# Both outer rows of a sampled attention summed on VectorE, row weights computed on GpSimd

## The reference, cut to what is computed

```python
x = x + _L0_conv_ref(_gn(x), Wq, Wk, Wv, off_w, off_b, attn_w, attn_b, Wo)
x = x + _L1_conv_ref(_gn(x), ...)

# in _L0_conv_ref: 8 heads of 8 channels, K2 = 9 taps
v = jnp.einsum('oc,nchw->nohw', Wv, x)
offsets = _conv2d(x, off_w, off_b)                    # 3x3, 144 channels
aw = jax.nn.sigmoid(_conv2d(x, attn_w, attn_b))       # 3x3, 72 channels
xp = (gx + 1.0) * 0.5 * (W - 1)                       # the pixel plus its offset
yp = (gy + 1.0) * 0.5 * (H - 1)
sampled = corner(y0, x0, wy0 * wx0) + corner(y0, x1, wy0 * wx1) + corner(y1, x0, wy1 * wx0) + corner(y1, x1, wy1 * wx1)
head_out = jnp.einsum('nhckxy,nhkxy->nhcxy', sampled, awr)   # summed over the taps k
return jnp.einsum('oc,nchw->nohw', Wo, combined)
```

## Time and profile before

| | us |
|---|---|
| Median of 3 runs (151.33 to 152.0) | 151.58 |
| Profiled execution, device time | 151.03 |
| Its span in the profile | 149.2 |
| Mean granted clock of TensorE, share of full | 0.976 |

### The profile page before, as it was taken

How to read it: one execution, slowest core, us unless ns; L and a number is a source line. 1 busy time by engine, 2 the same in 40 slices (tenths; PEclk the granted TensorE clock), 3 DMA queues, 4 the chain that set the end, 5 groups by cost and what they waited for, 6 DMA issues and landing times.

```text
span 149.2 us, 3269 instructions
## 1 busy us (share of the span) xinstructions
PE 129.2 (87%) x1395; PEld 111.3 (75%) x1395; DVE 110.5 (74%) x198; ACT 57.4 (38%) x102; POOL 18.5 (12%) x27
## 2 busy tenths in 40 slices
PE   4966399999999899999999998899887999797790
PEld 3654399998898889999899896687655667465460
DVE  5429895095459999799998999998757297965701
ACT  3009539837950768007880128012030317021100
POOL 8941120000000000000018000000003001030100
PEclk9999659999999999999999999999999999999999
DMA  3980000009964000000000000000000000000033
GB/s 95 271 152 0 0 0 4 0 15 256 244 120 108 19 7 0 0 0 4 0 0 0 0 4 0 0 0 4 0 2 4 4 0 4 0 4 0 0 75 70
DMA packets 6672, 5.48 MB, mean 37 GB/s; under 512 B 4656, under 2 KB 5938, under 8 KB 6658
## 3 DMA queue, kind: packets, MB, share of 16 engines
q1 hardware_dynamic: 5986, 4.26, 12.0%
q10 hardware_dynamic: 672, 1.02, 2.7%
HBM read 2.85 MB, written 0.52 MB: 23 GB/s over the span
## 4 chain that ended last, share of the span: by engine, by line
PE 50%; DVE 25%; issue 9%; DMA 6%; ACT 5%; SPq 1%; POOL 1%; POOLq 0%; DVEq 0%
PE bank L990 10%; PE bank L1009 9%; PE bank L982 8%; PE bank L1034 7%; DVE prod L742 7%; DMA prod<-in_w_off 6%; DVE part L769 3%; DVE x_t L861 3%; PE bank L1164 3%; PE bank L1131 3%; PE bank L959 2%; DVE wy L777 2%; DVE pooled L867 2%; DVE bn L580 2%; PE bank L943 2%
## 5 line engine op out<-in xcount | busy, mean ns | idle before, releaser
L742 DVE TENSOR_TENSOR prod<-hat,wy 128x1440 f32<-128x1440 f32 (+3 forms) x25 | 27.3, 1159 | 0.0
L769 DVE TENSOR_TENSOR part<-v,bank 128x1280 f32<-128x1280 f32 (+3 forms) x20 | 21.7, 1109 | 7.1 <-PE bank L1034 3.5
L1009 PE MATMUL bank<-cst,prod 128*128 128x128 f32 (+3 forms) x189 | 22.3, 272 | 0.8 <-DVE prod L742 0.8
L1034 PE MATMUL bank<-cst,part 128*128 128x128 f32 x168 | 21.1, 274 | 1.8 <-DVE part L769 1.4
L1009 PEld LDWEIGHTS bank<-cst,prod 128*128 128x128 f32 (+3 forms) x189 | 20.7, 131 | 1.4 <-DVE prod L742 1.0
L1034 PEld LDWEIGHTS bank<-cst,part 128*128 128x128 f32 x168 | 18.3, 140 | 3.2 <-DVE part L769 3.0
L943 PE MATMUL bank<-ones_r 128*128 128x512 f32 x67 | 18.5, 428 | 2.1 <-POOL w_pair L370 2.1
L990 PE MATMUL bank<-w_cross,g_cross 128*128 128x216 f32 x144 | 19.9, 285 | 0.0
L990 PEld LDWEIGHTS bank<-w_cross,g_cross 128*128 128x128 f32 x144 | 18.6, 203 | 0.0
L982 PE MATMUL bank<-w_pair,g_pair 128*128 128x216 f32 x96 | 15.3, 301 | 3.7 <-ACT g_cross L430 3.7
L943 PEld LDWEIGHTS bank<-ones_r 128*128 128x128 f32 x67 | 13.3, 207 | 4.9 <-POOL w_pair L370 2.1
(11 more groups left out here) (101 smaller groups left out, 154.9 us busy)
## 6 DMA issues: line engine op xcount, KB each, us to landing
v<-v SPq DMA_DIRECT2D x2, 480.0 KB, 6.2
v<-v SPq DMA_DIRECT2D x2, 448.0 KB, 5.9
prod<-in_w_off ACTq DMA_DIRECT2D x1, 486.0 KB, 7.0
prod<-in_w_off SPq DMA_DIRECT2D x1, 486.0 KB, 8.8
w_s<-in_w SPq DMA_DIRECT2D x4, 72.0 KB, 4.4
wc_s<-in_wc SPq DMA_DIRECT2D x2, 144.0 KB, 3.4
wp_s<-in_wp SPq DMA_DIRECT2D x4, 72.0 KB, 2.5
x_b<-in_x SPq DMA_DIRECT2D x1, 256.0 KB, 4.9
```

The source lines that it names most:

```text
L742: return nc.vector.tensor_tensor(prod[:, 0:K2 * CELLS * cx].rearrange("p (k q s) -> p q k s", k=K2, s=cx)[:, q0:q0 + nd], hat[:, c % 2, d0 ...
L769: nc.vector.tensor_tensor(part[:, n % PARTS, 0:nd, 0:cv].rearrange("p d (q e) -> p d q e", e=HD), moved, weights.unsqueeze(3).to_broadcast ...
L1009: last = nc.tensor.matmul(out_ps[0:size, b * P:(b + 1) * P], prod[:, at:at + size], ident, start=(b == 0 and t == 0), stop=(b == n - 1 and ...
L1034: last = nc.tensor.matmul(comb_bank[:, j * P:(j + 1) * P], part[:, n % PARTS, d, j * P:(j + 1) * P], ident, start=(m == 0 and d == 0 and j ...
```

## The change

- Rows 0 and 4 are both summed over their taps on DVE (`OWN_ROWS`, six cells). The reduction is replaced by four additions: taps 4 to 7 onto 0 to 3, taps 2 and 3 onto 0 and 1, tap 1 onto 0, and tap 8 with the sum into `cell`. The first three run in place in `prod`, each waiting for the one before.
- TensorE has two groups of tap sums. The projection of the chunk before stands between the transposes back of the two groups.
- `APPLY` is (4, 0, 2, 1, 3) in chunks 0 to 3 and stays (4, 2, 1, 3, 0) in chunk 4. The middle rows wait for the cells of both groups.
- The row weights `wy` of chunks 1 to 4 are computed by GpSimd once the weights `hat` are there and the second apply of the chunk before has ended; chunk 0's stay on DVE. DVE waits for them behind the edge reduction. GpSimd's clearing for the second block comes behind the last of them.
- On ScalarE all five distances and the far test of the next chunk come before the copies of the groups; the weights `hat` still come behind them.

```diff
+APPLY = ((4, 0, 2, 1, 3),) * (NC - 1) + ((4, 2, 1, 3, 0),)
-GROUPS = ((0, 8, 2), (8, 15, 3), (15, 18, 4))
-OWN_ROW = 4
-APPLY = (4, 2, 1, 3, 0)
+GROUPS = ((0, 8, 2), (8, 15, 3))
+SUMMED = 15
+OWN_ROWS = ROWS[3:]
+OWN = CELLS - SUMMED
...
+        def row_weights(engine, c):
+
+            x0, w = CHUNKS[c]
+            cx = w * HEADS
+            ck = K2 * cx
+            return engine.tensor_tensor(
+                wy[:, :, 0:ck].rearrange("p d (k q) -> p d k q", k=K2),
+                hat[:, c % 2, :, ck:2 * ck].rearrange("p d (k q) -> p d k q", k=K2),
+                mod[:, :, x0:x0 + w, :].rearrange("p k x h -> p k (x h)").unsqueeze(1).to_broadcast(
+                    [P, ND, K2, cx]), ALU.mult)
...
             nc.gpsimd.memset(wp_s[:, :, :, :], 0.0).then_inc(wp_zero, 1)
-            pool.wait_ge(off_ps, NC)
+            for c in range(1, NC):
+                pool.wait_ge(hat_ready, c + 1)
+                pool.wait_ge(mod_ready, c + 1)
+                pool.wait_ge(part_ready, ND * (c - 1) + len(OWN_ROWS))
+                row_weights(nc.gpsimd, c).then_inc(wy_ready, 1)
...
-            distances(1, 0, 1)
             for c in range(NC):
                 if c:
                     evacuate(c - 1)
-                    if c + 1 < NC:
-                        distances(c + 1, 0, 1)
+                if c + 1 < NC:
+                    distances(c + 1, 0, ND)
+                    far_tests(c + 1)
                 for g in range(len(GROUPS)):
                     copy_sums(c, g)
-                    if c + 1 < NC:
-                        distances(c + 1, g + 1, g + 2)
                 if c + 1 < NC:
-                    distances(c + 1, ND - 1, ND)
                     hats(c + 1)
...
-                for i in ROWS[:-1]:
+                ve.wait_ge(wy_ready, c + 1)
+                for i in ROWS[:3]:
                     product(i).then_inc(prod_ready, 1)
-                product(OWN_ROW).then_inc(hat_used, 1)
+                product(OWN_ROWS[0])
+                product(OWN_ROWS[1]).then_inc(hat_used, 1)
...
-                own_sum = tick(nc.vector.tensor_reduce(
...
+                taps = prod[:, 0:K2 * CELLS * cx].rearrange("p (k s) -> p k s", k=K2)[:, :, SUMMED * cx:]
+                link(nc.vector.tensor_tensor(taps[:, 0:4], taps[:, 0:4], taps[:, 4:8], ALU.add))
+                link(nc.vector.tensor_tensor(taps[:, 0:2], taps[:, 0:2], taps[:, 2:4], ALU.add))
+                link(nc.vector.tensor_tensor(taps[:, 0], taps[:, 0], taps[:, 1], ALU.add))
+                own_sum = tick(nc.vector.tensor_tensor(cell[:, :, 0:cx],
+                                                       taps[:, 0].rearrange("p (q s) -> p q s", s=cx),
+                                                       taps[:, 8].rearrange("p (q s) -> p q s", s=cx), ALU.add))
...
                 tap_sum(c, 0)
                 tap_sum(c, 1)
                 cells_back(c, 0)
-                tap_sum(c, 2)
-                cells_back(c, 1)
-                cells_back(c, 2)
                 if c:
                     y0(c - 1)
+                cells_back(c, 1)
```

## The result

| | before | changed |
|---|---|---|
| Median, us (4 runs each) | 151.46 | 154.8 (154.14 to 155.62) |
| Ratio, 95% interval | | 1.0264 (1.0156 to 1.0373) |
| Profiled execution, us | 151.03 | 154.14 |
| Its span, us | 149.2 | 152.3 |
| Mean granted clock | 0.976 | 0.955 |

A forecast was written before the change was run, and what follows sets the result against it. TensorE ends last in chunks 1 and 2, DVE in chunk 3. Chunk 3's products 2.1 us late, less 0.15, plus 0.3 in chunk 4, make 2.3 us: 151.58 + 2.3 = 153.9 us, range 151.3 to 156.6.

The forecast's parts named there:

- GpSimd's product of 1440 elements: Row weights of chunks 1 to 3 on GpSimd: 3.4 us each, against 1.65 on DVE.
- Work caught by the lower clock, its cost: TensorE behind chunk 0's gap: 4.2 us of work at the lower clock, costing 2.1 us.
- Products to second apply, chunk 4: Chunk 4: second apply 6.1 us behind the products, held by TensorE, where it was 5.76; 0.3 more.
- Part 4: ScalarE's five distances and far test ahead of the copies: TensorE stands still 3.7 us in chunk 0 and the clock falls.
- TensorE's lateness at chunk 1: TensorE free for chunk 1's tap sums at 52.1 instead of 48.26: 1.7 us late column plus 2.1 for the clock.
- All behind it is unchanged: Everything behind chunk 4's 0.3 us delay to the end of the kernel was to take the same time.
- Rival (b): Clock falls again in chunk 2's 1.9 us gap: another 2 us of TensorE time, 155.9 us; chance 0.10.
- Chunk 1's products: On DVE, they start at 47.2 instead of 45.8, behind GpSimd's product and the edge reduction.
- Rival (a): Clock stays at full through chunk 0's new gap: 2.1 us less, about 152.0 us; chance 0.22.
- Rival (c): Copies don't hold TensorE, DVE's period of 16.1 us counts: 2.5 us less, 149.1 us; chance 0.11.
- Rival (d): GpSimd's product outlasts its 4.8 us cover; at 6.5 us chunks 1 to 3 start later, near 157 us; chance 0.07.
- The lock between DVE and GpSimd: Between chunks, only the edge reduction (0.4 us) is held behind GpSimd's product; the three applies from PSUM are free.

The follow-up runs named there:

- experiment 1: Changed kernel with ScalarE's distances laid between the copies of the tap sums again, as in the kernel before: 149.81 us, ratio 0.986 to the kernel before.
- experiment 2: Kernel before with one part of the change alone, all five distances and the far test ahead of the copies: 160.81 us, ratio 1.0549.
- experiment 3: Changed kernel with 14 warming products in TensorE's gap before the first transpose back of chunk 0: 151.58 us, ratio 1.0016.
- experiment 8: Kernel of experiment 1 with shifted rows of v fetched in order 4, 0, 1, 3 and 8 instead of 10 warming products before chunk 4: 149.97 us.
- experiment 6: Changed kernel with the distances laid between the copies in chunk 0 alone: 151.02 us, ratio 0.9954.
- experiment 7: Changed kernel with the distances laid between the copies in chunks 1 to 3 alone: 151.23 us, ratio 0.9992.
- experiment 12: Kernel of experiment 1 once more, with more runs: 150.01 us, ratio 0.9862 to the kernel before, 12 runs.
- experiment 9: Kernel before with 17 instead of 10 warming products ahead of chunk 4: 152.49 us, ratio 1.0113.
- experiment 10: Changed kernel with 7 instead of 4 warming products between the two group means behind the last residual: 155.34 us, ratio 1.0135.
- experiment 11: Kernel of experiment 1 with 7 instead of 4 warming products between the two group means: 150.41 us, ratio 0.9886.
- experiment 4: Changed kernel with the row weights of every chunk back on DVE: 154.56 us, ratio 1.024.

## Why the prediction was right, point by point

The forecast for the median was 153.9 us, 2.3 above the kernel before; measured were 154.8 and 3.3 (3.1 between the profiles). Sign, mechanism and order of size are right, the size in part by luck; the parts are these.

| Step | forecast | measured |
|---|---|---|
| GpSimd's product of 1440 elements | 3.4 us | 3.28 |
| Products of chunk 1 start | 47.2 | 47.34 |
| First column behind the copies, chunk 0 | 40.25 | 40.08 |
| Work caught by the lower clock, its cost | 4.2, 2.1 us | 3.4, 1.6 us |
| TensorE free for chunk 1's tap sums | 52.1 | 51.3 |
| Column of chunk 1 | 58.4 | 57.64 |
| Column of chunk 2 | 76.95 | 76.14 |
| Products of chunk 3 (from 81.85) | 84.0 | 83.08 |
| Chunk 3 on DVE | 15.96 us | 15.93 |
| Products to second apply, chunk 4 | 6.1 us | 6.35 |
| Last residual (from 109.06) | 2.3 late | 1.6 late |
| Behind the last residual | unchanged | 1.5 us more |

- **Part 4, which the sum turned on, holds.** Experiments 1 and 2 show it from both sides: with the order undone the kernel is faster than before, and the order alone costs the kernel before 9 us. The fall of the clock was made by the gap (experiment 3).
- **The term that was mis-sized** is TensorE's lateness at chunk 1: 52.1 forecast, 51.3 measured. 0.5 of it is the clock's cost, 0.2 the first column; the columns and row sums between, less the 1.6 us of the clock, took 9.7 us as before. The clock's behaviour was read from the early gap, where it fell 2.1 us into the gap and stayed low for 6.8; here it fell at 40.0 us, 3.6 us after TensorE's last product and just behind the gap, and stayed low for 3.4, all of it on work. That 4.2 us of work came near 3.4 is luck. The 0.8 us go unchanged through the later steps of chunks 1 and 2; in chunk 4 another 0.3 came on top of the forecast.
- **"All behind it is unchanged" failed.** The code is, but the clock fell a second time and cost 1.5 us in the first branch convolution. Rival (b) had a second fall, in the gap of chunk 2 and at the price of 2 us; it came elsewhere, at 115 us. Two errors, 0.7 too much in the chunks and 1.5 too little behind, partly cancel: luck again.
- **Chunk 1's products** started at 47.34, forecast 47.2, but not for the reason given. The forecast let them wait for GpSimd; what ended last was chunk 0's last apply, which waited 1.28 us for TensorE's row sums.
- **Rival (a)** (full clock) gave 152.0; experiment 3, which keeps the clock up, has 151.58. **Rival (c)** gave 149.1 if the columns aren't held; experiment 1, where they aren't, has 149.8 to 150.0. Its DVE periods of 16.1 us were forecast with GpSimd covered; chunks 1 and 2 have 16.6 and 17.0, and the edge reductions held by GpSimd make up 0.75 and 0.9 us of them. **Rival (d)** didn't happen: in the changed kernel no product waits for GpSimd, not even chunk 1's.
- **The lock between DVE and GpSimd.** In the changed kernel the edge reduction starts at 46.96, after GpSimd's end at 46.30, so the two never met. Where it starts inside GpSimd's product it is held: 2.67 us instead of 0.45 in experiment 8 (43.42 + 3.27 = 46.69, the reduction ends at 47.01), 1.65 in experiment 1. This agrees with the Trainium skill, page "SBUF — State Buffer", section "Who interferes with whom", for an operation with two SBUF inputs; and the applies with one SBUF input and one in PSUM keep their 1.48 us.

**What stays open:** why the second fall comes, at 115 us in both profiles of the changed kernel. The first gap isn't needed for it: experiment 6 has no fall at 40 us and one at 115, and experiment 1, with no gap over 0.6 us before its transposes back, has one at 107.5. Nor does it always follow: the profile of experiment 7 has the gap and no late fall. In the mean clock a stay of 3.4 us weighs 0.011: 0.977 is the early stay of 6.8 us alone, 0.966 is 3.4 us more, 0.955 is 6.8 us more. All 8 executions of the changed kernel have 0.950 to 0.956; 8 of 10 have 0.976 or more with the gap filled (experiment 3), and 8 of 10 have 0.96 or more in experiment 7, where the gap alone accounts for 0.011. But 6 of 12 have 0.966 or less in experiment 12, without the gap, and 4 of the 22 executions of the kernel before that were pooled with experiments 9 to 12 have 0.966. So a late stay comes far more often with the change than before it, and no run shows by what; the short gap before the branch convolutions isn't shown to be the cause (experiments 9, 10).

## What to carry to other kernels

An engine that works in order and stands between two steps of another should do the short handing-over first and its own long work in the pauses: here five distances and a test ahead of two copies of 0.3 us turned a change worth 1.4% into a loss of 2.6%, of which the part behind the chunks, 1.5 us, has a cause that stays open. A gap on TensorE cost its length here only as far as it was longer than the other engines' chain (experiments 6 and 7), but it can cost again through the clock, so its length has to be looked at, not only its place. Moving an operation to a slower engine was free here while every DVE operation beside it had one input in PSUM, and the first with two SBUF inputs paid for it where GpSimd's product was still running (experiments 1 and 12).

## What the runs showed of the hardware

- A gap of 3.4 us on TensorE was followed by a fall of the granted clock in all six profiles that have it (the changed kernel twice, experiments 2, 4, 7 and 10): low for 3.4 us in five, for 6.8 in one. Filled with products that nobody needs, it left the clock at full (experiment 3).
- Shorter gaps sometimes did the same: 2.24 us in experiment 8, 1.77 us before the fall at 94 in experiment 4, 1.54 us before the fall at 60 in experiment 10. The changed kernel's gaps of 1.54 and 1.65 us were followed by none. Four profiles have a fall with no gap over 0.8 us in the 10 us before it: at 107.5 us (experiment 1), and at 115 (the changed kernel twice, experiment 6).
- A fall cost 1.5 to 1.7 us at 115, 3.4 us where it lasted 10 us (experiment 1), and nothing at 94, where DVE ended last. Without one, the stretch from the last residual to the end took 40.1 to 40.2 us in every profile.
- GpSimd's product of 1440 float32 elements with a broadcast operand took 3.26 to 3.30 us, twice DVE's 1.65; 720 elements took 1.72 to 1.74.
- DVE's edge reduction, two inputs in SBUF, took 0.45 us alone and 0.93 to 2.67 where it started inside a GpSimd product.
